# Last group of a two-matmul kernel in the exchanged layout, tile by tile; W and x loaded in another order

## The reference

```
w    = cond_weights[itok]                    # 64 matrices, 64 x 64
y    = einsum('bct,bcd->bdt', x, w)          # x: 64 x 64 x 512, f32
a, W'= quant_dequant_mxfp4(y), quant_dequant_mxfp4(W)   # per block of 32 along the last dim:
       # scale 2^(floor(log2 amax) - 2), values rounded to 0, .5, 1, 1.5, 2, 3, 4, 6 times it
out  = x + einsum('mk,nk->mn', a, W') + bias # W: 512 x 512
```

## Time and profile before

| | us |
|---|---|
| median of 3 runs | 98.38 |
| the profiled execution | 97.9 |
| its span, first to last instruction | 96.2 |
| PE busy | 84.4 |
| DVE busy | 81.9 |
| ACT busy | 75.3 |
| POOL busy | 32.9 |
| last add on DVE ends | 91.45 |

### The profile page before, as it was taken

How to read it: one execution, slowest core, us unless ns; L and a number is a source line. 1 busy time by engine, 2 the same in 40 slices (tenths; PEclk the granted TensorE clock), 3 DMA queues, 4 the chain that set the end, 5 groups by cost and what they waited for, 6 DMA issues and landing times.

```text
span 96.2 us, 2263 instructions
## 1 busy us (share of the span) xinstructions
PE 84.4 (88%) x715; PEld 41.2 (43%) x715; DVE 81.9 (85%) x138; ACT 75.3 (78%) x85; POOL 32.9 (34%) x60
## 2 busy tenths in 40 slices
PE   5999594999799998999899899989999989989800
PEld 4966252595482324344233433333352333445300
DVE  1248999999999999999999999999979999885600
ACT  4740498699998869999999999999999849957000
POOL 4273758399647548303000300320040021054000
PEclk9999999999999999999999999999999999999995
DMA  1898789694896789799999991896579399486992
GB/s 34 288 316 295 244 249 301 212 352 125 181 317 218 274 248 269 242 312 265 254 310 298 311 212 49 272 245 116 218 185 224 114 263 222 88 272 175 270 285 92
DMA packets 13901, 22.17 MB, mean 230 GB/s; under 512 B 4034, under 2 KB 4802, under 8 KB 13890
## 3 DMA queue, kind: packets, MB, share of 16 engines
q1 hardware_dynamic: 11456, 17.31, 56.4%
q0 software_dynamic: 2432, 4.73, 23.6%
q10 hardware_dynamic: 2, 0.00, 0.0%
HBM read 10.49 MB, written 8.39 MB: 196 GB/s over the span
## 4 chain that ended last, share of the span: by engine, by line
PE 44%; ACT 11%; DVE 10%; issue 6%; ACTq 0%; DVEq 0%
PE o_ps L357 20%; PE y_ps L357 5%; PE y_ps L306 5%; ACT y_sb L471 5%; ACT o_sb L493 4%; PE o_ps L352 4%; PE o_ps L337 3%; DVE a L654 3%; DVE n_int L625 2%; DVE top L645 2%; ACT z L463 1%; PE o_ps L382 1%; PE y_ps L367 1%; PE y_ps L300 1%; PE y_ps L318 1%
## 5 line engine op out<-in xcount | busy, mean ns | idle before, releaser
L357 PE MATMUL o_ps<-wT,aT 128*128 128x512 bf16 x100 | 23.8, 380 | 0.4 <-ACT aT L508 0.4
L183 POOL DMA_DIRECT2D mix<-in_L_cond_weights_dram x32 | 17.9, 560 | 12.4 <-issue 11.0
L625 DVE TENSOR_TENSOR n_int<-y_sb,inv 128x1024 int16<-128x1024 f32 (+1 forms) x17 | 19.5, 1155 | 0.2
L306 PE MATMUL y_ps<-x_sb,mix 64*64 64x512 f32 x120 | 15.6, 606 | 3.9 <-DMA mix<-in_L_cond_weights_dram 2.4
L272 POOL DMA_DIRECT2D x_sb<-o_sb x6 | 6.1, 1014 | 35.1 <-ACT o_sb L493 35.1
L382 PE MATMUL o_ps<-idle 128*128 128x128 bf16 x214 | 16.6, 235 | 1.2 <-DVE idle L664 1.2
L463 ACT ACTIVATE z<-y_ps 128x1024 bf16<-128x1024 bf16 x16 | 16.2, 1039 | 1.5 <-PE y_ps L306 1.2
L471 ACT COPY y_sb<-y_ps 128x1024 f32<-128x1024 f32 x16 | 16.3, 1035 | 0.0
L382 PEld LDWEIGHTS o_ps<-idle 128*128 128x128 bf16 x214 | 13.6, 105 | 5.1 <-issue 4.7
L480 ACT ACTIVATE zone<-inv 128x1024 int16<-128x1024 int16 (+2 forms) x11 | 11.6, 1074 | 3.8 <-DVE inv L618 3.8
L502 ACT COPY aT<-o_ps 128x1024 bf16<-128x1024 bf16 x14 | 13.7, 1045 | 1.0 <-PE o_ps L337 1.0
(11 more groups left out here) (52 smaller groups left out, 76.0 us busy)
## 6 DMA issues: line engine op xcount, KB each, us to landing
x_sb<-in_x_dram SPq DMA_DIRECT2D x7, 1024.0 KB, 6.4
out_dram<-x_sb SPq DMA_DIRECT2D x15, 256.0 KB, 3.6
x_sb<-o_sb POOLq DMA_DIRECT2D x6, 512.0 KB, 5.2
out_dram<-x_sb SPq DMA_DIRECT2D x6, 512.0 KB, 3.1
w_sb<-in_L_ffn_weight_dram SPq DMA_DIRECT2D x4, 256.0 KB, 3.4
x_sb<-in_x_dram SPq DMA_DIRECT2D x2, 512.0 KB, 6.6
out_dram<-x_sb POOLq DMA_DIRECT2D x4, 256.0 KB, 3.6
mix<-in_L_cond_weights_dram POOLq DMA_DIRECT2D x32, 16.0 KB, 4.5
```

Of the source, the lines that this page charges most:

```text
L183: queue.dma_start(mix[HALVES[i % 2], first + i // 2, :], table[bass.ds(row, 1), :, :].rearrange("o c d -> (o c) d")).then_inc(mix_in[step] ...
L306: last = nc.tensor.matmul(y_ps[HALVES[g], 2 * q + r, :], mix[HALVES[r], (step - 1) * GROUP + n, :], x_tiles(step, n)[HALVES[r], :], start= ...
L357: last = nc.tensor.matmul(o_bank(step, t), aT[:, t, c, :], wT[:, c, :], start=False, stop=(c == KC - 1))
L625: nc.vector.tensor_tensor(columns(n_int, t, n), columns(y_sb[:, step % 2, :, :], t, n), columns(inv, t, n), ALU.mult).then_inc(n_done, 1)
```

## The change

- SP issues the load of the conditions and W's tiles 1 and 3; ACT issues W's tiles 0 and 2, and x of group 1 after it has made z of the first two tiles of W.
- W is quantized in two pairs of tiles, each with its own inverse, zones, limit and rescale. PE turns W ahead of its second mix; 16, 24 and 48 idle matmuls stand where 24 and 60 stood.
- The row numbers are no longer tested for bounds as they are loaded.
- The last group is mixed in the exchanged layout throughout and stays in it: quantized, turned, copied and multiplied tile by tile. Its x comes from a second copy, `last_x`, in the exchanged layout, loaded by four DMAs behind SP's other loads; DVE adds into it and SP stores from it, one DMA for a tile (two halves of the columns for the last).
- In the group before the last, limit, rescale, turn and product go in pairs. Tiles 0 and 1 keep PE's add. Tiles 2 and 3 are turned back; tile 2 goes by `o_sb` and an accumulating DMA, tile 3 by an add on DVE.
- The store of group 6's tiles 2 and 3 goes from SP to POOL, behind two stores and an accumulating DMA of group 7.
- PSUM banks of the last two groups are dealt out anew.

```
+        last_x = sb("last_x", [P, GROUP, T], F32)
...
+        exchanged_x_dram = x.rearrange("(s q g r) c t -> s q g r c t", q=2, g=2, r=2)
...
+        def after(step):
+            return step + 2
+        def late_part(part):
+            return after(LAST - 1) + part
...
         def t_pair(step, q):
             if step < LAST - 1:
-                bank = 2 + q
-            else:
-                bank = 2 - q
-            return o_ps[:, bank, :].bitcast(BF16)
+                return o_ps[:, 2 + q, :].bitcast(BF16)
+            return y_ps[:, 3 - q, :].bitcast(BF16)
+        def t_last(t):
+            return o_ps[:, 1 + t % 2, :].bitcast(BF16)[:, 0:K]
         def o_bank(step, t):
             if step < LAST - 1:
                 return o_ps[:, t, :]
             if step == LAST - 1:
                 return y_ps[:, t, :]
-            return o_ps[:, 0, :] if t == 0 else y_ps[:, t - 1, :]
+            return (o_ps[:, 0, :], o_ps[:, 3, :], y_ps[:, 0, :])[t]
         def last_half(half):
-            return y_ps[:, 2 + half, 0:N // 2]
+            return y_ps[:, 1 + half, 0:N // 2]
...
-                cond_sb[:, 2 * first:2 * (first + len(tiles))], engines=[engine], min_val=0, max_val=S - 1)
+                cond_sb[:, 2 * first:2 * (first + len(tiles))], engines=[engine], min_val=0, max_val=S - 1,
+                skip_runtime_bounds_check_because="cond holds row numbers of the table")
...
-            for t in range(GROUP):
+            sp.dma_start(cond_sb[:, :], cond_row).then_inc(cond_in, 16)
+            for t in (1, 3):
                 load_w(sp, t)
-            for h in range(2):
-                sp.dma_start(x_tiles(1, 2 * h, 2).rearrange("p (n t) -> p n t", n=2),
-                             x_dram[:, 2 * h:2 * h + 2, :]).then_inc(x_first_in[h], 16)
             sp.wait_ge(cond_in, 16)
...
+            for t in range(GROUP):
+                sp.dma_start(last_x[:, t, :],
+                             exchanged_x_dram[LAST - 1, t // 2, :, t % 2, :, :]).then_inc(last_x_in, 16)
...
-                sp.wait_ge(x_added[step % 2], 16 * ((step + 1) // 2))
-                store(step, SUMMED, GROUP - SUMMED)
+                if step < LAST - 2:
+                    sp.wait_ge(x_added[step % 2], 16 * ((step + 1) // 2))
+                    store(step, SUMMED, GROUP - SUMMED)
+            sp.wait_ge(added, 1)
+            store(LAST - 1, GROUP - 1)
             for t in range(GROUP - 1):
-                sp.wait_ge(added, t + 1)
-                store(LAST, t)
+                sp.wait_ge(added, t + 2)
+                sp.dma_start(exchanged_dram[LAST - 1, t // 2, :, t % 2, :, :],
+                             last_x[:, t, :]).then_inc(stored, 16)
             for half in range(2):
-                sp.wait_ge(added, GROUP + half)
-                sp.dma_start(out_dram[:, TILES - 1, n_half(half)], x_tiles(LAST, GROUP - 1)[:, n_half(half)]
+                sp.wait_ge(added, GROUP + 1 + half)
+                sp.dma_start(exchanged_dram[LAST - 1, 1, :, 1, :, n_half(half)],
+                             last_x[:, GROUP - 1, n_half(half)]
                              ).then_inc(stored, 16)
-            sp.wait_ge(stored, 16 * (3 * (LAST - 2) + GROUP + 1))
-            sp.wait_ge(late_stored, 16 * 2 * 2)
+            sp.wait_ge(stored, 16 * (3 * (LAST - 2) - 1 + 1 + GROUP + 1))
+            sp.wait_ge(late_stored, 16 * 4)
...
-            for q in range(2):
-                pool.wait_ge(late_copied, 2 * q + 2)
-                for g in range(2):
-                    pool.dma_start(exchanged_dram[LAST - 2, q, g, :, :, :].rearrange("r c t -> c r t"),
-                                   x_tiles(LAST - 1, 2 * q, 2)[HALVES[g], :].rearrange("p (r t) -> p r t", r=2)
-                                   ).then_inc(late_stored, 16)
+            pool.wait_ge(late_copied, 2)
+            for g in range(2):
+                pool.dma_start(exchanged_dram[LAST - 2, 0, g, :, :, :].rearrange("r c t -> c r t"),
+                               x_tiles(LAST - 1, 0, 2)[HALVES[g], :].rearrange("p (r t) -> p r t", r=2)
+                               ).then_inc(late_stored, 16)
+            pool.wait_ge(late_tile, 1)
+            pool.dma_start(x_tiles(LAST - 1, SUMMED), o_sb[:, (LAST - 1) % 2, 0, :], accum_op=ALU.add
+                           ).then_inc(x_added[(LAST - 1) % 2], 16)
+            pool.wait_ge(x_added[(LAST - 2) % 2], 16 * ((LAST - 1) // 2))
+            n0 = (LAST - 3) * GROUP + SUMMED
+            pool.dma_start(out_dram[:, n0:n0 + 2, :], x_tiles(LAST - 2, SUMMED, 2).rearrange("p (n t) -> p n t", n=2)
+                           ).then_inc(late_stored, 16)
+            pool.wait_ge(x_added[(LAST - 1) % 2], 16 * (LAST // 2))
+            n0 = (LAST - 2) * GROUP + SUMMED
+            pool.dma_start(out_dram[:, n0, :], x_tiles(LAST - 1, SUMMED)).then_inc(late_stored, 16)
...
-                if step == LAST and q == 1:
-                    for n in (2 * q, 2 * q + 1):
-                        for half in HALVES:
-                            last = nc.tensor.matmul(y_ps[half, n, :], mix[half, (step - 1) * GROUP + n, :],
-                                                    x_tiles(step, n)[half, :], start=True, stop=True)
-                        last.then_inc(y_ready, 1)
-                    return
...
+            def bias_half(half):
                 row = half * 32
                 nc.tensor.matmul(last_half(half), ones[row:row + 3, :], bias3[row:row + 3, n_half(half)],
                                  start=True, stop=False)
...
-                pe.wait_ge(a2_done, LAST + t + 1)
-                if t == 3:
-                    pe.wait_ge(aT_ready, tiles_done(LAST, 1))
+                pe.wait_ge(a2_done, late_part(2 + t))
+                if t >= 2:
+                    pe.wait_ge(aT_ready, tiles_done(LAST, t - 2))
...
+            def zone_pair(inverses, limits, t0=0, n=2):
+                act.wait_ge(inv_done, inverses)
+                if limits > 0:
+                    act.wait_ge(top_done, limits)
                 nc.scalar.activation(columns(zone, t0, n).bitcast(I16), columns(inv, t0, n).bitcast(I16), ACT.Copy,
                                      bias=float(EXPONENT - 2 * BINADE), scale=-1.0).then_inc(zone_done, 1)
...
+            def copy_late_tile():
+                act.wait_ge(x_added[(LAST - 1) % 2], 16 * ((LAST - 2) // 2))
+                act.wait_ge(o_ready, tiles_done(LAST - 1, SUMMED))
+                nc.scalar.copy(o_sb[:, (LAST - 1) % 2, 0, :], o_bank(LAST - 1, SUMMED)).then_inc(late_tile, 1)
...
             for q in range(2):
                 mix_pair(1, q)
+            keep_busy(16)
+            for q in range(2):
+                pe.wait_ge(a2_done, q + 1)
+                turn_pair(0, q, straight=True)
             keep_busy(24)
             for q in range(2):
                 mix_pair(2, q)
-            pe.wait_ge(ident_ready, 1)
-            for q in range(2):
-                pe.wait_ge(a2_done, q + 1)
-                turn_pair(0, q, straight=True)
-            keep_busy(60)
+            keep_busy(48)
             mix_pair(3, 0)
...
+            for q in range(2):
+                ffn_pair(LAST - 2, q)
             pe.wait_ge(y_copied, tiles_done(LAST, 3))
-            residual_pair(LAST - 1, 1)
-            for t in range(GROUP):
+            pe.wait_ge(a2_done, late_part(0))
+            turn_pair(LAST - 1, 0, straight=True)
+            residual_pair(LAST - 1, 0)
+            for t in range(2):
                 bias_tile(LAST - 1, t, start=False)
+            pe.wait_ge(a2_done, late_part(1))
+            turn_pair(LAST - 1, 1)
+            for t in range(2):
+                ffn_tile(LAST - 1, t)
+            pe.wait_ge(aT_ready, tiles_done(LAST - 1, 3))
+            for t in range(2, GROUP):
+                bias_tile(LAST - 1, t)
+            for t in range(2, GROUP):
+                ffn_tile(LAST - 1, t)
+            pe.wait_ge(pair_copied, 2 * (LAST - 2))
             bias_tile(LAST, 0)
-            for t in range(GROUP):
-                ffn_tile(LAST - 1, t)
-            pe.wait_ge(a2_done, LAST + 2)
-            turn_pair(LAST, 0)
+            turn_last(0)
+            pe.wait_ge(copied_out, 2 * (LAST - 2))
+            turn_last(1)
+            bias_tile(LAST, 1)
             pe.wait_ge(late_copied, 2)
-            bias_tile(LAST, 1)
             bias_tile(LAST, 2)
             ffn_tile(LAST, 0)
             turn_last(2)
             ffn_tile(LAST, 1)
             turn_last(3)
+            bias_half(0)
+            pe.wait_ge(late_tile, 1)
+            bias_half(1)
             ffn_tile(LAST, 2)
...
-            act.dma_start(cond_sb[:, :], cond_row).then_inc(cond_in, 16)
+            for t in (0, 2):
+                load_w(act, t)
             act.wait_ge(ones_ready, 1)
             nc.scalar.activation(table_loaded[:, :], ones[0:3, :], ACT.Abs)
-            for t in range(GROUP):
+            for t in range(2):
                 z_w(t)
-            zone_group(0)
```

(161 more changed lines are left out.)

97 lines of the change are left out of this document (34 added, 63 removed).

## The result

| | before | changed |
|---|---|---|
| median, us | 98.25 (97.59 to 98.47, 4 runs) | 123.86 (123.28 to 124.41, 4 runs) |
| profiled execution's span | 96.2 | 121.6 |

The ratio is 1.262, 95% interval 1.252 to 1.272: 26% slower, at the upper side of the forecast (120; 113 to 129).

The account below looks back on a forecast made before the run. DVE, PE and ACT are full mid-kernel, so only start, tail and transfers move time. Last-group transfers on two DMA engines give span 118.5, plus 1.7 is 120.2: 120 us, 113 to 129 (8 in 10: 96.5 to 128).

Parts of the forecast that it names:

- Bound and spread: Compute engines full mid-kernel; new last-group transfers, outermost count 2, run on two DMA engines, 5.4 us a tile; chance 0.70.
- Size of the stores: Last group's stores on two engines: 21.7 us, replacing 2.7 us of that group's work as spread over 16.
- a store's fixed part: Last group's stores: a store's landing time less its packets, taken as 1.6 us in the lower end of the span.
- What is left over at 82 us: Work of the second x's loads still queued on the two engines at 82 us: nothing to 15.5 us.
- the end that has nothing left over: Lower end of the two-engine span: first last-group store at 88, plus 1.6 and 21.7, giving 111.3 us.
- SP's stalls: SP may stall issuing the new loads, but was said to hold only stores that end before the last ones.
- The sum: Two-engine span 118.5 plus 1.7 us around it, 120.2; median said as 120, range 113 to 129.
- Start: Quantizing W in pairs delays its second inverse and z of group 1: +0.8 us, bounds +0.3 to +1.5.
- Tail: Last group tile by tile: last rescale at 85.8, last add at 89.5, 2.0 us earlier, before the start's shift.
- the first rival: All 16 engines carry the new transfers; last stores end at 95.1, time 97.5, 96 to 98.6; chance 0.26.
- the second: All 16 engines, start's loss of 1.5 passed on in full, tail's gain lost in the stores: 99.4; chance 0.04.

Follow-up runs that it names:

- experiment 4: Kernel before plus four spare 256 KB loads at the end of SP's list, outermost counts 128, 8, 4, 2, each awaited: 117.14 us in one execution.
- experiment 2: Changed kernel with only the four loads of the second x issued by halves of the rows, last five stores as they were: 117.24 us, ratio 1.192.
- experiment 3: Changed kernel with only the last group's five stores issued by halves of the rows, loads as they were: 104.05 us once, 105.88 to 105.91 in three.
- experiment 1: Changed kernel with all nine transfers (four loads, five stores) issued by halves, 64 rows outermost: 99.77 us, ratio to the kernel before 1.012.
- experiment 5: Changed kernel with the nine transfers by halves and the start of the kernel before, bounds test still off: 99.96 us, ratio 1.017.
- 8: Changed kernel with transfers by halves, last stores from SP and ACT, tile 2 of group 7 by DVE, old start: 96.52 us, ratio 0.982.
- experiment 9: Changed kernel with transfers by halves, tile 2 of group 7 by DVE, old start, last ten store issues all from SP: 98.59 us, ratio 1.002.
- 10: The fastest kernel (halves, two store queues, tile 2 by DVE, old start) with the row numbers' bounds test put back: 96.80 us, ratio 0.984.
- experiment 7: Changed kernel with halves and two store queues, tile 2 of group 7 added by DVE without accumulating DMA or last POOL store: 97.95 us, ratio 0.992.
- 6: Changed kernel with transfers by halves, five of the last ten store issues from ACT instead of SP: 100.03 us, ratio 1.019.

## Why the prediction was right, and where it was not

**Bound and spread.** This was right, and it is the mechanism, not only the number. The count of closing packets, seen before only for 1, 64 and 128, holds for 2, 4 and 8 (experiment 4). The Trainium skill, "DMA: Bandwidth & Descriptors", section "Why a DMA increments its semaphore by 16 and not by 1", has the largest number up to 16 that divides both outermost sizes; by this rule 2, 4 and 8 were due, and these runs agree.

**Size of the stores.** 21.7 less 2.7, which is 19.0, was said, 17.5 measured. The kernel compared with already waits 7.9 us for its stores instead of 4.8 (below), and these hide part of the two engines' time; that this is the whole difference was not tried. The 1.6 us taken for a store's fixed part don't come out of the rows: they give 3.1 - 16 x 0.085 = 1.7 to 3.6 - 8 x 0.085 = 2.9.

**What is left over at 82 us.** The bounds were 0 and 15.5, and 118.5 lies 7.2 above the end that has nothing left over. Measured are 6.6 by the difference of times (experiment 2) and 4.3 to 6.1 (experiment 3). That the middle of wide bounds came so near is in part luck. SP reached the loads at 31.75 (said: 35), and no compute engine waited for them (DVE 47.68 of 48 us from 34 to 82). One step was priced too low: SP's stalls were said to hold only stores that end before these. In fact SP issues the first store of `last_x` at 90.47, against 88.49 in experiment 1.

**The sum.** With the forecast's own terms it is 118.5 + 1.7 + 0.5 = 120.7, not 120. Measured were 123.86: the kernel with 16 engines took 2.3 more than its price of 97.5, and the two engines cost 24.1 where 120 - 97.5 = 22.5 was said. Both errors have the same sign and are small beside 24.

**Start.** +0.8 was said. The beat's product stands at 55.94 instead of 54.99: +0.95. The steps of the changed kernel, in order of time:

```profile
12.51 0.43 DVE L668 TENSOR_SCALAR inv<-low 128x1024 int16<-128x1024 int16 x1
...
12.97 1.06 ACT L512 ACTIVATE zone<-inv 128x1024 int16<-128x1024 int16 x1 [3.92 <-DVE inv L668]
...
13.94 1.92 ACT L496 ACTIVATE z<-y_ps 128x1024 bf16<-128x1024 bf16 x2
...
15.88 0.69 DVE L628 TENSOR_TENSOR m<-z 128x1024 bf16<-128x1024 bf16 x1 [1.07 <-ACT z L496]
...
16.49 0.68 DVE L703 TENSOR_TENSOR a<-n_int,top 128x1024 bf16<-128x1024 int16 x1
```

The second inverse ends at 12.94 (said 12.8), its zone holds up z of group 1 as the forecast had it, DVE waits 1.07 us for it, and W's last rescale ends at 17.17 (said 17.3), against 16.58. The steps came as said, but the runs don't show that they cost time: with the old start under otherwise the same list (experiments 5, 8 and 9) W's last two tiles come late instead. DVE waits 1.6 to 2.1 us for them where it waited 1.34 (the forecast gave this wait to the third tile; the instruction takes both), and the last rescale ends at 16.90 to 17.32. The kernel before without the bounds test has no such delay (it waits 1.37 us); why the others have it is open. Not foreseen: in experiment 1 the first mix fell into a stretch of low granted clock:

```profile
11.85 3.45 PE L332 MATMUL y_ps<-x_sb,mix 64*64 64x512 f32 x16 [1.29 <-DMA mix<-in_L_cond_weights_dram]
12.00:14.00 2.00, 2.00 (x12) 0.71 (x12) 1.97 (x5) 1.17 (x2) 1.85 (x3) 0.54 1.08 298
```

The granted clock is 0.54 in these 2 us: it falls from the full level to the lower one, 0.50. The mix took 3.45 us where it takes 1.95 in the changed kernel, after PE had idled 1.29 us for the matrices; the profile of the changed kernel idled 1.30 and kept its clock. The last add came 0.6 later, at 90.69. The profiles of experiments 2 and 10 have the same stretch (3.45 and 3.64 us), the others have not, though PE idled up to 1.54 us there (experiment 3). So idle time alone does not tell when it comes, and what it does to the medians was not tried apart.

**Tail.** For the end of compute 90.3 was said with the start's shift, and 90.09 measured. The last inverse ends at 80.92 and the last rescale at 86.65 (said, with the shift: 81.3 and 86.6).

**What failed: the first rival's price,** "3.05 MB need 10.6 us, from about 84.5: 95.1". With 16 engines the same kernel took 99.8, not 97.5. The step counted bytes at a mean rate. Measured in its place: from the last add at 90.69 the stores of experiment 1 took 7.9 us to the end of the span, against 4.8 before. The order of its last POOL and SP issues:

```profile
84.44 1.30 POOL L301 DMA_DIRECT2D out_dram<-x_sb  x2 [2.59 <-ACT x_sb L532]
85.73 0.99 POOL L305 DMA_DIRECT2D x_sb<-o_sb  x1
86.34 1.13 POOL L309 DMA_DIRECT2D out_dram<-x_sb  x1
91.03 0.57 POOL L313 DMA_DIRECT2D out_dram<-x_sb  x1 [3.56 <-DMA x_sb<-o_sb]
```

```profile
88.49 5.72 SPq L247 DMA_DIRECT2D out_dram<-last_x  x6
94.26 2.51 SPq L252 DMA_DIRECT2D out_dram<-last_x  x4
```

The sum had the bytes of one more accumulated tile, but not what they cost in time at the engines and in the store that waits for them (experiment 7: 2.1 us with two queues). Nor had it a price for the issues, ten on one queue where five went before (experiment 9: 2.1 us). The two costs overlap and don't add up: taking away both, with the new start, gives 99.77 - 97.95 = 1.8. From the last add to the end of the span it is 7.9 us in experiment 1, 8.4 in 6, 7.3 in 9, 6.0 in 7 and 5.1 in 8, against 4.8 before. So the tail's gain in compute was real and was spent in the stores; with both costs away and the start undone 96.5 is reached. Of the forecast's cases with 16 engines the second, 99.4 with the tail's gain lost in the stores, came nearest to the 99.77, and it had a chance of 0.04; its other half, a loss of 1.5 at the start, is not borne out by experiment 5, and experiments 7 and 8 leave it open.

## What to carry to other kernels

Put the 64 or 128 rows outermost on both sides of a transfer; when one side has to be cut in two, issue two transfers. Closing packets (the packets of a queue less the rows moved) tell from the profile of a kernel how many engines its transfers use, so a new shape can be tried by a spare load as in experiment 4. An end that waits for stores is not shortened by faster compute alone: price the issues and the accumulating transfers behind the last add as well.

## What was not expected of the hardware

A transfer on two engines does harm beyond its own time. SP's issue of it blocks: 0.5 to 7.9 us each for the four loads, 5.0 for the last two stores. Other transfers land later: the last accumulating one in 12.5 us instead of 5.0 (experiment 3 against 1). An issue has a price of its own, 0.60 us for a half store of the exchanged layout and 0.35 for a plain tile. In the tail neither a second issuing queue alone (100.03 against 99.77) nor less DMA work on one queue (98.59) reached 96.5; both together did.
